# Half-wise drive buffers, reciprocals taken from a reshaped copy in memory, and a shorter end of the recall stage

## The chip, the cores and the metric

The kernel runs on one core of one Trainium2 chip. The metric is the device time of one execution in microseconds (us); lower is better. PE is TensorE (matmuls and transposes), PEld its weight loads, DVE VectorE, ACT ScalarE, POOL GpSimd, SP SyncE, which issues most DMAs.

## The reference

Eight images of 1024 tokens and 32 text tokens (`B` = 8, `SEQ` = 1056, width `D` = 64) pass through a Fourier patch embedding, attention, a mixture of 16 experts, a linear recurrent attention and a mixture of 8 experts. The change lies in the recurrent attention and at its seam to the last experts. Cut to what matters:

```python
def step(carry, v_prev):                       # over time, 1056 steps, n = 256 neurons
    x_update = relu(v_prev @ Dx.T)
    x_t = 0.97 * x_state + x_update
    x_t = x_t / max(sum(abs(x_t)), 1e-12)
    a_star = einsum('bdn,bn->bd', rho, x_t)
    y_t = relu(_ln(a_star) @ Dy.T) * relu(x_t)
    v_star = _ln(y_t @ E.T)
    rho_t = 0.97 * rho + _ln(v_prev)[:, :, None] * x_t[:, None, :]
    return (x_t, rho_t), v_star
h = h + _L1_attn_ref(_layernorm(h), E, Dx, Dy)
h = h + _L1_ffn_ref(_layernorm(h), ...)        # 8 experts, the best 2 of each token
```

## The kernel before

The program is a row of blocks with a barrier of all engines between two of them: nothing of a block starts before every engine has finished the block ahead. Inside a block each engine runs its own list in the order in which it is written, and waits on semaphores. Four blocks matter here.

**First experts** (`main` of `moe_phase`, tiles `d_...`), up to 1328 us. It ends before the input of the last two images is normalised.

**Drive** (`drive_block`). For each pair of images `pr` (0 to 3) the normalised rows are transposed on PE (`turn`, three pieces `i` through one bank `p_turn`) and copied by ACT (`keep`) into `vT`. For each of three chunks `a` of 352 columns PE forms `Dx @ v` (`drive`) into the four banks of `p_u`, and ACT applies the relu (`relu`) and writes `x_all`. `drive(pr, a)` fills all four banks at once: `p_u[:, q, f]`, `q` being the image of the pair and `f` the half of the 256 neurons; each `relu` reads the two banks of one image. DVE adds the two neuron halves (`join`), PE sums over neurons (`add_up`), and from that sum DVE works out the divisor of every time step (`level`, parts 0 to 7): a scaling, a comparison, a scan over time, two more operations, and four reciprocals of a quarter row each. It does so for images 0 and 1 here (`EARLY` = 2, rows on 2 partitions) and for images 2 to 7 (6 partitions) in the next block. SP writes the reciprocals to memory (`rate_scr`) and spreads them over 128 partitions (`spread_rate`), and DVE scans each image's half with them (`scan_drive`). On POOL `feed_drive(B - 1)` normalises the last image, after DVE has measured it (`feed_measure(g, dve, feed, 1, B - 1)` and `feed_gather`); PE's `turn(3, 0)` waits for it. The relus of the last pair wait for the end of the early levels, since these borrow rows of images 6 and 7.

**Recall** (`recall_answer_block`). A loop over `n`, with `b, t = divmod(n, 9)`, a tile of 128 tokens each: PE scores tile `n + 1` against itself, DVE masks it (`mask`, tile `k_pm`), PE weighs the values (`weigh`, tile `k_p_a`), and updates the state (`keep_state`). Score and mask buffers are two deep. Two images behind, `turn_la`, `core`, `gate` and `answer` make the output of image `b - 2`; DVE and POOL normalise and add it three images behind (`v_rows`, `v_moment`, `v_add`). In images 0 and 1 of the loop the cores and answers are still missing, and the late levels and the scans of images 1 to 3 stand in DVE's list. In its last rounds the block prepares image 0 of the second experts: `normalise`, `double`, `turn_tokens`, `logits`, `rank`, `choose`, `turn_gates`, `keep_gates`, then SP's `spread_out` and `spread_in` of the gates. POOL's last step is `v_add(7)`; the barrier waits for it.

**Second experts** (`main` of `moe_phase`, tiles `n_...`): 96 groups `i` of a first and a second layer on PE, from 1630 us to the end.

## Time and profile before

| | |
|---|---|
| median of 3 runs | 1944.66 us (1934.02 to 1953.28) |
| profiled execution, its own time | 1941.79 us |
| its span, first to last instruction | 1940.0 us |
| mean granted TensorE clock | 0.947 of full speed |
| PE busy | 1747.2 us (90%) |
| DVE, ACT, POOL busy | 1265.1, 1043.6, 348.9 us |
| first experts end, drive begins | 1328.8 us |
| drive ends, recall begins | 1390.7 us |
| recall ends, second experts begin | 1629.7 us |

All moments are counted from the first instruction of the profiled execution. Busy shares are means over stages with different limits; a change within drive and recall is to be read in the stretch from 1328 to 1634 us, and there in PE's idle time and its clock.

### The profile page before, as it was taken

To read this page: it belongs to the slowest core of one execution; us is meant where nothing else is said; L and a number is where in the kernel's file an instruction comes from. 1 tells how busy PE (TensorE), PEld (TensorE's weight loads), DVE (VectorE), ACT (ScalarE), POOL (GpSimd) and SP (SyncE) were. 2 spreads that over 40 slices of the span, in tenths; PEclk is the share of its full clock that TensorE was granted. 3 is DMA by queue.
4 is the path that set the end of the run, shared out by engine and by line. 5 is a ranking of instruction groups with operands and counts; after the bars stand their busy time and mean duration, and the time that the engine had idled before them with its cause. 6 is when DMAs were issued, how large, how long until landed. Compare 5 with 4: busy or idle time off the path is not lost. (4 is left out here: it accounts for less than half of the span.)

```text
span 1940.0 us, 41019 instructions
## 1 busy us (share of the span) xinstructions
PE 1747.2 (90%) x15480; PEld 756.6 (39%) x15480; DVE 1265.1 (65%) x3165; ACT 1043.6 (54%) x1974; POOL 348.9 (18%) x332
## 2 busy tenths in 40 slices
PE   5866899999999999999989999997899987999998
PEld 2331222222222222222324444443488974444443
DVE  1447888888888788878715687875666662434431
ACT  1330477777777677767764555554323332555554
POOL 1222100000000000000101345546113443000000
PEclk9975799999999899989999999998979997999999
DMA  5624022121212112110127576440110002332241
GB/s 189 230 76 73 2 35 47 35 46 36 45 37 42 40 34 48 29 36 19 35 63 155 105 135 131 92 91 18 34 58 13 1 2 46 71 79 52 58 87 22
DMA packets 89057, 118.74 MB, mean 61 GB/s; under 512 B 30892, under 2 KB 71942, under 8 KB 86814
## 3 DMA queue, kind: packets, MB, share of 16 engines
q1 hardware_dynamic: 84266, 106.93, 25.9%
q0 software_dynamic: 3104, 8.72, 1.3%
q8 instruction: 126, 2.06, 0.5%
q14 instruction: 69, 0.57, 0.1%
q10 hardware_dynamic: 1492, 0.46, 0.1%
HBM read 97.26 MB, written 18.82 MB: 60 GB/s over the span
## 5 line engine op out<-in xcount | busy, mean ns | idle before, releaser
L843 ACT ACTIVATE b_prob<-b_p_s 128x512 f32<-128x512 f32 x1104 | 570.4, 603 | 285.3 <-PE b_p_s L1012 269.8
L866 DVE TENSOR_REDUCE b_m<-b_p_m 128x1 f32<-128x1024 f32 x512 | 604.0, 1219 | 122.8 <-PE b_p_s L1012 87.7
L1012 PE MATMUL b_p_s<-b_q,b_k 51*64 51x512 bf16 x2048 | 347.9, 400 | 11.2 <-ACT b_prob L843 11.2
L967 PE MATMUL b_p_m<-b_k,b_q 48*64 48x512 bf16 x1656 | 301.5, 421 | 53.7 <-DMA b_k<-qk_scr 22.5
L1040 PE MATMUL b_p_o<-b_prob,v_all 128*9 128x512 f32 x2304 | 300.2, 603 | 0.9
L967 PEld LDWEIGHTS b_p_m<-b_k,b_q 48*64 48x64 bf16 x1656 | 75.1, 108 | 373.7 <-DVE b_m L866 233.2
L1414 ACT ACTIVATE d_hidden<-d_p_z 128x704 f32<-128x704 f32 x192 | 135.1, 754 | 103.0 <-PE d_p_z L1324 102.8
L1414 ACT ACTIVATE n_hidden<-n_p_z 128x704 f32<-128x704 f32 x192 | 135.0, 754 | 99.4 <-PE n_p_z L1324 99.2
L821 POOL DMA_DIRECT2D sum_scr<-b_sums x48 | 26.3, 548 | 747.5 <-ACT b_sums L833 723.7
L1552 DVE TENSOR_TENSOR d_xg<-d_xd,d_c_wide 128x352 f32<-128x352 f32 x192 | 113.1, 625 | 67.1 <-PE d_p_z L1324 32.9
L1324 PE MATMUL d_p_z<-d_xg,d_w 64*128 64x352 f32 x768 | 143.0, 488 | 0.6 <-DVE d_xg L1552 0.6
L1324 PE MATMUL n_p_z<-n_xg,n_w 64*128 64x352 f32 x768 | 142.2, 486 | 0.0
L1337 PE MATMUL d_p_y<-d_hidden,d_w 128*64 128x352 f32 x768 | 135.4, 474 | 0.0
L1337 PE MATMUL n_p_y<-n_hidden,n_w 128*64 128x352 f32 x768 | 134.6, 472 | 0.0
L1012 PEld LDWEIGHTS b_p_s<-b_q,b_k 51*64 51x64 bf16 x2048 | 92.0, 105 | 54.0 <-ACT b_prob L843 46.7
L1324 PEld LDWEIGHTS d_p_z<-d_xg,d_w 64*128 64x128 f32 x768 | 69.6, 188 | 48.9 <-ACT d_hidden L1414 23.1
L1324 PEld LDWEIGHTS n_p_z<-n_xg,n_w 64*128 64x128 f32 x768 | 69.3, 187 | 48.3 <-ACT n_hidden L1414 22.0
L1337 PEld LDWEIGHTS d_p_y<-d_hidden,d_w 128*64 128x64 f32 x768 | 47.0, 137 | 77.0 <-issue 63.3
L1552 DVE TENSOR_TENSOR n_xg<-d_xn_all,m_x_all 128x352 f32<-128x352 f32 x96 | 47.5, 518 | 44.8 <-PE n_p_z L1324 18.6
L1337 PEld LDWEIGHTS n_p_y<-n_hidden,n_w 128*64 128x64 f32 x768 | 46.7, 136 | 76.1 <-issue 62.3
L967 PE MATMUL b_p_m<-b_k_head,b_q_head 48*64 48x512 bf16 x392 | 63.1, 403 | 7.0 <-ACT b_prob L843 7.0
L2186 ACT ACTIVATE k_state<-k_p_r 128x128 f32<-128x128 f32 x64 | 17.7, 277 | 87.5 <-PE k_p_r L2111 86.6
(362 smaller groups left out, 2212.2 us busy)
## 6 DMA issues: line engine op xcount, KB each, us to landing
d_c_wide<-d_c_scr SPq DMA_DIRECT2D x48, 704.0 KB, 13.4
m_x_all<-n_c_scr SPq DMA_DIRECT2D x48, 352.0 KB, 8.2
xt<-in_x SPq DMA_DIRECT2D x16, 1024.0 KB, 8.7
sum_scr<-b_sums POOLq DMA_DIRECT2D x32, 256.0 KB, 2.8
b_q<-qk_scr SPq DMA_DIRECT2D x96, 66.0 KB
qk_scr<-a_qk_part SPq DMA_DIRECT2D x24, 256.0 KB, 2.8
k_rate<-rate_scr SPq DMA_DIRECT2D x8, 528.0 KB, 4.2
b_k<-qk_scr SPq DMA_DIRECT2D x16, 198.0 KB
```

What stands on the lines that cost most here:

```text
L821: pool.dma_start(g.sum_scr[b, p, :, a * WIDE:a * WIDE + w], sums[:, n % 2, 0:w]).then_inc(sum_sent[n % 2], 16)
L843: nc.scalar.activation(prob[:, U % PR_RING, 0:w], p_s[:, U % S_RING, 0:w], ACT.Exp, scale=float(D) ** -0.5).then_inc(exp_done, 1)
L866: nc.vector.tensor_reduce(m3[:, x, 0:1], p_m[:, s, :, :].rearrange("p k n -> p (k n)"), axis=AX.X, op=ALU.max).then_inc(rows_free, 1)
L967: last = nc.tensor.matmul(out[e:e + 64, k, :], q[:, t * P + e:t * P + e + 64], keys[:, k * WIDE:k * WIDE + WIDE], start=True, stop=True)
L1012: last = nc.tensor.matmul(out[e:e + 64, :], k_st[s][r, q, jt * P + e:jt * P + e + 64], q_st[s][r, q, a * WIDE:a * WIDE + WIDE], start=True ...
L1040: last = nc.tensor.matmul(p_o[32 * i:32 * i + DH + 1, :], v[:, jt, p * QUAD + i, :], prob[:, slot, :], start=(jt == 0), stop=(jt == FULL), ...
L1324: last = nc.tensor.matmul(own["p_z"][:, n % 2, q, 0:CH], w1[r, pr, f * P:f * P + P], own["xg"][r, n // HALVES % XR, :], start=True, stop=True)
L1337: last = nc.tensor.matmul(own["p_y"][q * D:q * D + D, 0:CH], w2[:, 2 * pr + q, f, :], own["hidden"][:, n % HR, q, :], start=(k == 0), stop ...
L1414: nc.scalar.activation(own["hidden"][:, n % HR, :, :], own["p_z"][:, n % 2, :, 0:CH], ACT.Relu).then_inc(relu_done, 1)
L1552: nc.vector.tensor_tensor(own["xg"][:, j % XR, :], own["xd"][b % 3][:, a * CH:a * CH + CH], own["c_wide"][b % 2][a][:, pr, :], ALU.mult)\
L2186: nc.scalar.mul(state[:, :, :].rearrange("p f d -> p (f d)"), p_r[:, 0:2 * D], DECAY ** -2).then_inc(held, 1)
```

## The change

Five things: (1) `drive(pr, a, f)` fills two banks, those of one neuron half, and `relu` reads them; PE fills the one half while ACT reads the other, with the transposes between the halves. (2) The levels stop after part 3. SP writes the divisors to memory and reads them back as rows of 66 elements on 32 (early) or 96 (late) partitions, DVE takes one reciprocal of that (`invert_levels`), SP writes it to `rate_scr`. (3) In drive, the statistics of the last image stand ahead of the levels, the scans of image 0 ahead of `join(6)` and `join(7)`, and `add_up(4)` and `add_up(5)` one chunk earlier. (4) In recall, the late levels fill rounds 0 to 3 in one row, the scans of image 1 move to rounds 4 and 6. (5) At recall's end both halves of `answer(6)` go ahead of `turn_la(7, ...)`, `normalise(1)`, `double(1)`, `turn_gates(0)` and `keep_gates(0)` go later, and the normalisation and addition of the last answer moves behind the barrier, into the second experts' block.

```diff
+            if answers:
+                answer_add(g, pool, answers, B - 1)
             rstd_of(2)
...
+                    if answers and i == 2:
+                        answer_rows(g, dve, answers, B - 1, range(NT))
+                    if answers and i == 3:
+                        answer_moments(g, dve, answers, B - 1)
+                    if answers and i == FIRST_GROUP[B - 1] - 4:
+                        dve.wait_ge(answers["v_step"], 5 * B)
...
+def load_levels(g, sp, k, lo, hi, level, part):
+    sp.wait_ge(k["level"], LEVEL_STEPS * (part + 1))
+    sp.dma_start(k["den_scr"][lo:hi, :], level).then_inc(k["den_sent"], 16)
+    sp.wait_ge(k["den_sent"], 16 * (part + 1))
+    sp.dma_start(k["den"][0:(hi - lo) * SPREAD, :], k["den_scr"][lo:hi, :].rearrange("b (s n) -> (b s) n", s=SPREAD)).then_inc(k["den_in"], 16)
+def send_rates(g, sp, k, rate_scr, lo, hi, part):
+    sp.wait_ge(k["inverted"], part + 1)
+    sp.dma_start(rate_scr[lo:hi, :].rearrange("b (s n) -> (b s) n", s=SPREAD), k["inverse"][0:(hi - lo) * SPREAD, :]).then_inc(k["rate_sent"], 16)
+    sp.wait_ge(k["rate_sent"], 16 * (part + 1))
+def invert_levels(g, dve, k, lo, hi, part):
+    dve.wait_ge(k["den_in"], 16 * (part + 1))
+    if part:
+        dve.wait_ge(k["rate_sent"], 16 * part)
+    n = (hi - lo) * SPREAD
+    g.nc.vector.reciprocal(k["inverse"][0:n, :], k["den"][0:n, :]).then_inc(k["inverted"], 1)
+LEVEL_STEPS = 6
+SPREAD = 16
...
-            def drive(pr, a):
-                n = NC * pr + a
+            def drive(pr, a, f):
+                n = 2 * (NC * pr + a) + f
                 pe.wait_ge(vT_ready, 3 * pr + 3)
-                pe.wait_ge(relu_done, 2 * n)
-                for f in range(2):
-                    for q in range(2):
+                if n >= 2:
+                    pe.wait_ge(relu_done, n - 1)
+                for q in range(2):
...
-                    drive(pr, a)
+                    drive(pr, a, 0)
                     if pr + 1 < TWOS:
                         turn(pr + 1, a)
+                    drive(pr, a, 1)
...
-                    if pr == 3 and a >= 1:
-                        add_up(3 + a)
+                    if pr == 3 and a < 2:
+                        add_up(4 + a)
...
-                    act.wait_ge(k["level"], LEVEL_STEPS)
+                    act.wait_ge(k["den_sent"], 16)
...
             join(0)
             join(1)
+            feed_measure(g, dve, feed, 1, B - 1)
+            feed_gather(g, dve, feed, 1, B - 1)
             dve.wait_ge(summed, EARLY)
             for part in (0, 1, 2):
                 level(part)
-            feed_measure(g, dve, feed, 1, B - 1)
-            feed_gather(g, dve, feed, 1, B - 1)
             join(2)
             level(3)
             join(3)
-            for part in (4, 5, 6, 7):
-                level(part)
-            for b in range(4, B):
-                join(b)
+            invert_levels(g, dve, k, 0, EARLY, 0)
+            join(4)
+            join(5)
             for f in range(2):
                 scan_drive(g, dve, k, u_all, 0, f)
+            join(6)
+            join(7)
...
-            for b in range(B + 3):
+            for b in range(B + 2):
...
-            pool.wait_ge(v_step, 5 * B)
...
+                if b == B and t == 7:
+                    for half in range(2):
+                        answer(b - 2, half)
...
+                if n == AFTER + 9:
+                    turn_gates(0)
...
-                if n == AFTER + 5:
+                if n == AFTER + 9:
                     normalise(1)
```

In drive, PE's list from the first product of pair 0 into pair 1 (`h_p_u` the drive, `h_p_turn` a transpose, `k_trio<-...f_column` an `add_up`), before:

```order
L1865 MATMUL h_p_u<-k_yT,k_xr 128x352 x4
L1855 MATMUL h_p_turn<-eye,d_xn_all 128x128 x4
L1865 MATMUL h_p_u<-k_yT,k_xr 128x352 x4
L1855 MATMUL h_p_turn<-eye,d_xn_all 128x128 x4
L1865 MATMUL h_p_u<-k_yT,k_xr 128x352 x4
```

and after the change:

```order
L1899 MATMUL h_p_u<-k_yT,k_xr 128x352 x2
L1889 MATMUL h_p_turn<-eye,d_xn_all 128x128 x4
L1899 MATMUL h_p_u<-k_yT,k_xr 128x352 x4
L1889 MATMUL h_p_turn<-eye,d_xn_all 128x128 x4
L1899 MATMUL h_p_u<-k_yT,k_xr 128x352 x4
```

The transposes stand inside a chunk now, after two of its four products; a row of four is the second half of one chunk and the first of the next.

In drive, DVE's list from the first two joins (`k_a_sb<-m_x_all`, `k_laT<-m_x_all`) to the barrier, before (`f_st`, `f_mv` the last image's statistics, `m_x_all<-m_x_all,k_rate` the scans of image 0):

```order
L1785 SCALAR_TENSOR_TENSOR k_v_sb<-k_rate,m_x_all 2x1056
L1684 BN_STATS f_st<-hid 128x6 x9
L1693 BN_AGGR f_mv<-f_st 128x2 x9
L1947 TENSOR_TENSOR k_a_sb<-m_x_all 128x1056
L1789 SCALAR_TENSOR_TENSOR m_x_all<-k_v_sb,m_x_all 2x1056
L1791 TENSOR_SCALAR m_x_all<-m_x_all 2x1056
L1947 TENSOR_TENSOR k_laT<-m_x_all 128x1056
L1795 RECIPROCAL k_rate<-m_x_all 2x264 x4
```

and after, the same stretch with what stands ahead of it:

```order
L1692 BN_STATS f_st<-hid 128x6 x9
L1701 BN_AGGR f_mv<-f_st 128x2 x9
L1792 TENSOR_SCALAR m_x_all<-k_trio 2x1056
L1793 MEMSET k_v_sb 2x1
L1796 TENSOR_SCALAR k_rate<-m_x_all 2x1056
L1799 SCALAR_TENSOR_TENSOR k_v_sb<-k_rate,m_x_all 2x1056
L1981 TENSOR_TENSOR k_a_sb<-m_x_all 128x1056
L1803 SCALAR_TENSOR_TENSOR m_x_all<-k_v_sb,m_x_all 2x1056
L1805 TENSOR_SCALAR m_x_all<-m_x_all 2x1056
L1981 TENSOR_TENSOR k_laT<-m_x_all 128x1056
L1829 RECIPROCAL k_inverse<-k_den 32x66
```

The statistics are ahead of the whole level, and one reciprocal of 66 elements a row stands where four of 264 stood.

At recall's end, PE's list from `core(6, 5)` to `core(7, 0)` (`k_trio<-eye,k_la` is `turn_la`, `k_eT,k_yT` is `answer`, `n_cw` is `turn_gates`), before:

```order
L2129 MATMUL k_p_s<-k_laT,k_dyT 128x352
L2120 MATMUL k_trio<-eye,k_la 64x128 x3
L2138 MATMUL k_trio<-k_eT,k_yT 128x64 x10
L2120 MATMUL k_trio<-eye,k_la 64x128 x3
L2138 MATMUL k_trio<-k_eT,k_yT 128x64 x8
L1298 MATMUL k_p_t<-eye,n_cw 64x128
L1299 MATMUL k_p_t<-eye,n_cw 8x128
L2120 MATMUL k_trio<-eye,k_la 64x128 x3
L2129 MATMUL k_trio<-k_laT,k_dyT 128x352
```

and after:

```order
L2181 MATMUL k_p_s<-k_laT,k_dyT 128x352
L2190 MATMUL k_trio<-k_eT,k_yT 128x64 x18
L2172 MATMUL k_trio<-eye,k_la 64x128 x9
L1300 MATMUL k_p_t<-eye,n_cw 64x128
L1301 MATMUL k_p_t<-eye,n_cw 8x128
L2181 MATMUL k_trio<-k_laT,k_dyT 128x352
```

Both halves of answer 6 stand ahead of the three transposes of image 7, and the transposes of the gates behind them.

## Rows read from the trace of the kernel before

**Rows 1.** Stretch, length, busy PE, PEld, DVE, ACT, POOL, granted clock, DMA share, GB/s

```profile
1328.80:1390.50 61.70, 47.67 (x192) 21.37 (x192) 34.06 (x74) 24.61 (x43) 20.39 (x16) 0.85 0.12 32
1391.00:1403.00 12.00, 11.77 (x103) 11.34 (x103) 10.44 (x13) 5.31 (x14) 1.56 (x4) 1.00 0.21 46
1403.00:1415.00 12.00, 8.97 (x73) 7.51 (x71) 11.66 (x21) 3.61 (x11) 0.00 (x0) 1.00 0.01 3
1417.00:1431.00 14.00, 14.00 (x67) 13.92 (x66) 3.93 (x7) 2.60 (x8) 1.35 (x1) 0.50 0.35 116
1596.50:1608.40 11.90, 10.20 (x47) 9.10 (x47) 3.21 (x35) 2.34 (x7) 5.75 (x5) 0.50 0.02 5
```

**Rows 2.** Timeline of drive: start us, us, engine, line, operation, idle before

```profile
1343.38 2.30 POOL L1725 TENSOR_TENSOR hid<-hid,d_xn_all 128x576 f32<-128x576 f32 x1
1343.82 1.46 PE L1865 MATMUL h_p_u<-k_yT,k_xr 64*128 64x352 f32 x8 [1.39 <-ACT k_yT L1913]
1345.20 0.66 PE L1855 MATMUL h_p_turn<-eye,d_xn_all 128*128 128x128 f32 x4
1345.32 1.41 ACT L1919 ACTIVATE m_x_all<-h_p_u 128x704 f32<-128x704 f32 x2 [1.55 <-PE h_p_u L1865]
1353.85 1.20 DVE L1684 BATCH_NORM_STATS2 f_st<-hid 128x6 f32<-128x64 f32 x9
1358.14 0.70 DVE L1791 TENSOR_SCALAR m_x_all<-m_x_all 2x1056 f32<-2x1056 f32 x1
1362.42 1.09 PE L1855 MATMUL h_p_turn<-eye,d_xn_all 128*128 128x128 f32 x4 [5.38 <-POOL d_xn_all L1710]
1388.52 1.94 PE L1872 MATMUL k_trio<-k_laT,f_column 128*6 128x352 f32 x6
```

**Rows 3.** SP's issues of the early rates, and DMA issue to landing

```profile
1366.73 0.23 SPq L1832 DMA_DIRECT2D rate_scr<-k_rate  x1
1368.11 0.82 SPq L1762 DMA_DIRECT2D k_rate<-rate_scr  x2
DMA to landing us min/median/max: 3.6/4.2/5.5
```

**Rows 4.** The late reciprocals on DVE: min/median/max in ns, first and last start

```profile
L1795 DVE RECIPROCAL k_yT<-k_yT x4: 1792/1792/1793, 1405.6 to 1412.4; 6x264 f32<-6x264 f32 x4
```

**Rows 5.** Timeline of recall's first two images: weighing on PE, DVE

```profile
1396.01 0.33 PE L2099 MATMUL k_p_a<-v_all,k_pm 128*128 128x64 f32 x2
1397.79 0.33 PE L2099 MATMUL k_p_a<-v_all,k_pm 128*128 128x64 f32 x2
1415.21 0.53 PE L2099 MATMUL k_p_a<-v_all,k_pm 128*128 128x64 f32 x2 [0.73 <-DVE k_pm L2250]
1418.63 0.53 PE L2099 MATMUL k_p_a<-v_all,k_pm 128*128 128x64 f32 x2
1436.04 2.35 DVE L1767 TENSOR_TENSOR_SCAN m_x_all<-m_x_all,k_rate 128x1056 f32<-128x1056 f32 x1
1442.06 0.28 DVE L2250 TENSOR_TENSOR k_pm<-k_p_s,k_tri 128x128 f32<-128x128 f32 x1
```

**Rows 6.** Timeline of recall's end and the start of the second experts

```profile
1592.16 0.76 DVE L1471 TENSOR_TENSOR v_all<-v_all,n_rs 128x576 f32<-128x576 f32 x1 [1.97 <-POOL n_rs L1252]
1596.54 0.85 PE L2120 MATMUL k_trio<-eye,k_la 128*64 128x128 f32 x3 [5.08 <-DVE k_la L2284]
1608.41 1.54 PE L2129 MATMUL k_trio<-k_laT,k_dyT 128*128 128x352 f32 x2 [0.56 <-ACT k_laT L2191]
1616.22 0.21 POOL L2037 TENSOR_TENSOR k_v_mv<-k_v_mv,eps 128x9 f32<-128x9 f32 x1 [10.21 <-DVE k_v_mv L2296]
1620.89 1.40 POOL L2045 TENSOR_TENSOR hid<-hid,k_v_sb 128x576 f32<-128x576 f32 x1
1627.84 1.40 POOL L2045 TENSOR_TENSOR hid<-hid,k_v_sb 128x576 f32<-128x576 f32 x1
1629.97 1.11 PE L1283 MATMUL n_p_g<-eye,m_x_all 128*128 128x128 f32 x4 [10.15 <-POOL n_yT L1255]
```

More of the change, by code:

```diff
@@ L1553, in scale, with main @@
                     .then_inc(gated, 1)
-        def main():
+        def main(answers):
             scale(0)
@@ L1599, in vector_steps, with main @@
         return measure, gather, normalise, rank, choose, main
-    def main(chunks, stale):
+    def main(chunks, stale, answers=None):
         with ExitStack() as c2:
@@ L1629, in _ @@
                 _, _, _, run = pool_steps(pool)
-                run(stale)
+                run(stale, answers)
             @block.tensor
@@ L1644, in _ @@
                 _, _, _, _, _, run = vector_steps(dve)
-                run()
+                run(answers)
     return own, main, (sync_steps, pool_steps, tensor_steps, scalar_steps, vector_steps)
@@ L1744, in feed_recall, with recall_buffers @@
     feed_normalise(g, pool, feed, 2, n + 3, feed["vn"][:, b, :, :], feed["sums"][b])
-def recall_buffers(g, c):
+def recall_buffers(g, c, late):
     sb = lambda n, s: c.enter_context(g.nc.sbuf_tensor("k_" + n, s, F32))
+    keep = lambda n, s: late.enter_context(g.nc.sbuf_tensor("k_" + n, s, F32))
+    v_sb, v_st, v_mv = keep("v_sb", [P, 2, NT, D]), keep("v_st", [P, NT, 6]), keep("v_mv", [P, NT, 4])
     return {"rate": sb("rate", [P, RATES, SEQ]), "tri": sb("tri", [P, P]), "fade": sb("fade", [P, 2, NT]),
@@ L1791, in level_of @@
         nc.vector.tensor_scalar(scaled, scaled, L1_EPS / DECAY, None, ALU.max).then_inc(step, 1)
-    if part >= 4:
-        dve.wait_ge(step, n0 + 6)
-        cols = slice((part - 4) * SEQ // 4, (part - 3) * SEQ // 4)
-        nc.vector.reciprocal(small[:, cols], scaled[:, cols]).then_inc(step, 1)
-LEVEL_STEPS = 10
+def load_levels(g, sp, k, lo, hi, level, part):
[15 more added lines that the diff above has]
+SPREAD = 16
 def drive_block(g, u_all, feed, rate_scr, k, p_sum, own, steps):
@@ L1830, in _ @@
             load_experts()
-            sp.wait_ge(k["level"], LEVEL_STEPS)
-            sp.dma_start(rate_scr[0:EARLY, :], early["small"]).then_inc(rate_sent, 16)
-            sp.wait_ge(rate_sent, 16)
+            load_levels(g, sp, k, 0, EARLY, early["scaled"], 0)
+            send_rates(g, sp, k, rate_scr, 0, EARLY, 0)
             for b in range(EARLY):
@@ L1926, in _ @@
                 for a in range(NC):
-                    for q in range(2):
-                        relu(pr, a, q)
+                    relu(pr, a, 0)
                     if pr + 1 < TWOS:
                         keep(pr + 1, a)
+                    relu(pr, a, 1)
                     if (pr, a) == (1, 1):
@@ L2010, in _ @@
             load_biases()
-            sp.wait_ge(kb["level"], 2 * LEVEL_STEPS)
-            sp.dma_start(rate_scr[EARLY:B, :], late["small"]).then_inc(rate_sent, 16)
-            sp.wait_ge(rate_sent, 16)
+            load_levels(g, sp, kb, EARLY, B, late["scaled"], 1)
+            send_rates(g, sp, kb, rate_scr, EARLY, B, 1)
             for b in range(EARLY, B):
@@ L2228, in _ @@
                     soften(0)
-                if n == AFTER + 8:
-                    keep_gates(0)
                 if 1 <= b <= B and t >= 7:
@@ L2234, in _ @@
                     laT_copy(b - 2, 2)
+                if n == AFTER + 9:
+                    keep_gates(0)
                 if b < B:
@@ L2305, in _ @@
             mask(0)
-            for n in range(NT * (B + 3)):
+            for n in range(NT * (B + 2)):
                 b, t = divmod(n, NT)
@@ L2320, in _ @@
                     gather(1)
-                if n == AFTER + 5:
+                if n == AFTER + 9:
                     normalise(1)
@@ L2419, in all_stages @@
         with ExitStack() as c3:
-            buffers = recall_buffers(g, c3)
+            buffers = recall_buffers(g, c3, c)
             trio = c3.enter_context(nc.psum_tensor("k_trio", [P, 3, 512], F32))
@@ L2423, in all_stages @@
             recall_answer_block(g, x_all, vn_all, rate_scr, feed, buffers, trio, own, steps)
-        second_experts((), ())
+        second_experts((), (), buffers)
 def build(nc, arg, const, out, stages):
```

111 lines of the change are left out of this document (54 added, 57 removed).

## The prediction

> **What bounds the kernel now.** I read the busy shares by stretch first, then the timeline of PE's waits, then DVE, POOL and SP around them. The experts and the attention stage, some 1600 of the 1940 us, keep PE busy and are not touched. The change lies where PE waits. Drive lasts 61.7 us and PE is busy for 47.67 of them, so 14.0 us are idle, and the clock's mean of 0.85 says that it stood at 1.2 GHz for three tenths of the stretch [rows 1]. Recall's first two images are bound by DVE from 1403 to 1415 (DVE 11.66 of 12.00 us busy, PE 8.97), and right after that the clock stands at 1.2 GHz with PE busy without a gap, 14.00 of 14.00 us [rows 1]. At recall's end PE waits for DVE, runs at 0.50 [rows 1], and idles while POOL adds the last answer; those numbers follow below.
>
> **Drive: buffers by half.** Before, a chunk's four products take 1.46 us and the two relus behind them 1.41 us, one after the other, since PE needs all four banks back: the row of 1343.82 shows PE waiting 1.39 us for ACT, and ACT in turn waiting 1.55 us for PE [rows 2]. With halves, PE has 1.46 + 0.66 (four transposes) = 2.1 us a chunk and ACT its relus and a copy of about the transposes' length, 1.41 + 0.6 = 2.0 us, beside each other. Only the two joins' `add_up` (1.94 us each) still hold PE for data. **The moved statistics.** The last image is ready on POOL at 1343.38 + 2.30 = 1345.7, but DVE measures it at 1353.85, behind the level's scan, and PE waits 5.38 us for POOL's result, until 1362.42 [rows 2]. Put ahead of the level, the measuring starts at about 1346, so POOL is done after the same 1362.42 - 1353.85 = 8.6 us, at 1354.6, or sooner, since the two instructions that ran slowly there ran beside DVE's joins. PE gets there at about 1353. The price is 2 us more before the level; as `add_up(1)` ends only at about 1348, DVE would have waited through those 2 us anyway.
>
> **Drive: the levels through memory.** The early level is ready for the reciprocals at 1358.14 + 0.70 = 1358.8 [rows 2], and the rates leave at 1366.73 [rows 3]: 7.9 us, of which a join and four reciprocals. Written over 32 partitions a row has 66 elements, a quarter of 264. At the duration per element of the late ones, 1.79 us for 264 [rows 4], one reciprocal of 66 takes an estimated 0.45 us; from below it is not under the 0.28 us of a mask [rows 5], from above not over 1.79. It adds two DMAs, out and back. The only row alike is the write of the rates, 1368.11 - 1366.73 = 1.4 us until SP was released [rows 3]; the read may take up to the 4.2 us of a landing [rows 3], though it moves 8 KB and not 528. I take 1.4 + 2.0 + 0.5 = 3.9 us in place of 6.9 on this path. The level itself comes some 3 us earlier, at 1355.7, as its sum does. Rates then land at 1355.7 + 3.9 + 1.4 + 4.2 = 1365.2. The relus of the last pair no longer wait for reciprocals, only for the first write (1357).
>
> **Drive: the sum.** Walked through in the new order, with `add_up(1)` ending at 1348 (pair 0 runs mostly at the low clock and gains about 1 us) and the other two chunks of pair 1 at 1352: pair 2 takes three chunks of 2.1 and two `add_up` of 1.94, 10.2 us, to 1362; pair 3, without transposes, three of 1.46 and two of 1.94, 8.3 us, to 1370; DVE's two scans (2.35 us each, [rows 5]) run from 1366 to 1371 and are through when the last relus end (1371); joins 6 and 7 to 1374; `add_up(7)` ends at 1378 instead of 1388.52 + 1.94 = 1390.5 [rows 2]. **Drive gives 12 us.** By the other way round: 14.0 us idle less about 4 that stay (the first copies, the joins) and plus 2 of a cold stretch that no longer occurs is the same 12. Bounds 8 (halves worth nothing beyond the moved statistics and level) and 15 (no idle left, no low clock but the first).
>
> **Recall's start.** DVE's list loses four reciprocals of 1.79 us, 7.2 us, and gains 0.45. The scans of image 1 move behind the level. Between two masks at most 2.4 us of other work stand, three times in a row (rounds 2 to 4), against PE's pace of 1397.79 - 1396.01 = 1.78 us a tile [rows 5]: with buffers two deep that costs about 1 us once. Before, PE lost 12.00 - 8.97 = 3.0 us there [rows 1], so 2 us are saved at the least. The rest hangs on the clock. The tiles come every 1418.63 - 1415.21 = 3.42 us after the fall and 1.78 before [rows 5]. The fall came after the stretch in which PE was busy for 75%; the twelve us before it, of the same tiles at 98%, kept 2.4 GHz [rows 1]. Without the gaps I expect it to stay. Then DVE becomes the bound at rounds 15 to 18: four scans of 2.35 us, the centring and scaling, statistics and masks, about 13 us for what PE does in 8. Followed through, the mask that stands at 1442.06 [rows 5] comes 10 us earlier, not 14. **I take 10**, bounds 3 (clock falls as before) and 13. The late rates pass three DMAs of 1.4 to 4.2 us and one spread of 4.2; the scan that needs them is six rounds, 11 us, behind the reciprocal, so they cost nothing.
>
> The Trainium skill's page "TensorE: Matmul & The Clock Gate", part 1, says that sustained activity releases the throttle; by that the stretch from 1417 would have been short, and this term only 2 us. The trace doesn't agree: the clock stayed at 0.50 through 14.00 us without an idle moment [rows 1].
>
> **Recall's end.** `normalise(1)` no longer stands ahead of the last gates, so DVE doesn't wait 1.97 us for POOL there [rows 6]; with its own two instructions of 0.76 gone, what stands behind comes 3.5 us sooner, gate (6, 5) near 1593. PE's 5.08 us of idling [rows 6] shrink to some 1.6, then answer 6 fills PE, and the three transposes of image 7 with their copies are no longer held up by ACT's `keep_gates`, which waited for the gates' transposes. `core(7, 0)` starts at 1605 instead of 1608.41 at the low clock, at 1601 if it stays high. From it the last gate takes the 7 us of before, then DVE's moments, and POOL's addition of answer 6: 1616.22 to 1620.89 + 1.40 = 1622.3, 6.1 us [rows 6]. That is now the end: 1619 (low) or 1613 (high), where before POOL went on to 1627.84 + 1.40 = 1629.2 [rows 6]. So 10 or 16 us; 6.9 of them are the last addition alone. I take **10**, since the clock was already low in [rows 1] at 1596.5 and a pause of 1.6 us behind a thin stretch may suffice. The addition in the next block costs PE nothing: DVE has about 2 us more and POOL 6.1, and the next statistics that POOL must finish come two groups (6 us) later than the moments. SP's gates leave about as early as before and the first chunk has landed when the block starts; bound 2 us.
>
> **Sum.** 1941.8 - 12 - 10 - 10 = 1909.8. The profiled execution is 2.9 us below the median of three, which spread by 19 us, so I make it **1910 us**.
>
> **Rivals.** (a) *The clock falls in recall's start anyway*, say because most of these products move only 64 columns: the term is 3 and not 10, 1917 us. For it: at 0.50 the same tiles, without a gap, brought no rise in 14 us [rows 1]; against it: the 98% stretch. Chance 0.33 against 0.37 for the forecast. The same page, part 4, says that transposes don't count as busy in the same way, and recall is full of them; that speaks for this rival, and no run here parts transposes from thin products. (b) *The clock stays high at the end too*: 6 us more and a warm start of the experts, 1903 us; chance 0.17. (c) *Halves don't do what they say*: PE in drive is held by joins, levels and rates, not by buffers; drive gives 8 or less, 1914 to 1918; chance 0.08. (d) *Slower*: the clock, low from a place in recall on, does not come back with the products of 352 columns. Each tile at 3.42 and not 1.78 costs 1.64 us, so from 32 / 1.64 = 20 low tiles more than before it eats everything. Images 2 to 7 have them in every tile; 0.02. (e) The round trips through memory take the reciprocals' place as the wait: each us beyond the 1365 of the rates delays the scans, joins 6 and 7 and the barrier by the same; at 4.2 us each for three DMAs drive gives 6; 1916, chance 0.03.
>
> **The numbers.** Range 1896 to 1925: from (b) with drive at 15 to (a) with drive at 8, and the spread of the runs. About 1% (19 us) is what a measurement of this kernel can tell from no change. All cases but (d) and an unforeseen one lie below 1925; with both terms of the clock at their worst and the early bounds (8 + 3 + 7 = 18) it is within 1%. Faster 0.92, same 0.06, slower 0.02.
>
> **What would show it.** In drive: ACT's and PE's rows overlapping, no wait of PE on POOL, last `add_up` at about 1378. In recall: no run of waits of PE on `k_pm` in the first nine tiles, clock 1.0 at 35 to 40 us from recall's start; one 96-row reciprocal of about 0.5 us. At the end: the barrier about 10 us after the last gate's core, PE's idle time ahead of the second experts 3 to 4 us and not 10.15. The forecast is wrong if the clock falls at another place, or if DVE's rows of statistics in the experts make PE wait.

## The result, and the profile after

| | before | changed |
|---|---|---|
| median | 1944.2 us (4 runs, 1934.0 to 1953.3) | 1917.8 us (4 runs, 1915.1 to 1926.4) |
| ratio to before, 95% interval | | 0.9858 [0.9815, 0.9900] |
| span of the profiled execution | 1940.0 us | 1914.3 us |
| drive, first transpose to recall's first DMA issue | 61.9 us | 55.1 us |
| recall, to the second experts' first product | 239.2 us | 217.2 us |
| ... its start to the mask of tile 20 | 51.3 us | 41.3 us |
| ... from there to the last mask | 135.3 us | 135.3 us |
| ... from the last mask to the second experts | 52.7 us | 40.6 us |
| second experts | 310.0 us | 311.2 us |

The spans differ by 25.7 us: 6.8 in drive, 22.1 in recall, less 1.2 lost in the second experts and 2.1 by which the unchanged blocks ahead of drive were later in this execution. The forecast was 1910 in 1896 to 1925. The gain is 1.4%, and the interval of the ratio lies below 1. Here and below the ratios leave out a few executions that ran at a lower clock, so that they are not always the quotient of the medians.

Busy time by stretch in the changed kernel, columns as in [rows 1]: drive, recall's two first twelve us, the low stretch, the end.

```profile
1330.80:1385.90 55.10, 47.39 (x192) 19.71 (x192) 29.89 (x71) 25.43 (x43) 23.39 (x16) 0.86 0.13 36
1386.30:1398.30 12.00, 11.77 (x103) 11.25 (x102) 9.75 (x13) 5.31 (x14) 1.50 (x4) 1.00 0.22 48
1398.30:1410.30 12.00, 11.60 (x104) 10.91 (x103) 7.07 (x30) 4.53 (x14) 2.02 (x2) 1.00 0.32 95
1418.00:1424.00 6.00, 6.00 (x29) 5.15 (x30) 4.62 (x7) 2.18 (x6) 0.00 (x0) 0.50 0.24 90
1580.00:1592.00 12.00, 10.65 (x42) 8.11 (x42) 3.80 (x20) 3.43 (x8) 6.29 (x5) 0.51 0.01 4
```

Drive has 7.7 us of idle PE in place of 14.0, but the mean clock is 0.86 and not near 1. Its timeline, which answers to [rows 2]:

```profile
1346.33 2.29 POOL L1733 TENSOR_TENSOR hid<-hid,d_xn_all 128x576 f32<-128x576 f32 x1
1352.96 4.14 POOL L1716 TENSOR_TENSOR d_xn_all<-hid,f_mv 128x576 f32<-128x576 f32 x1
1357.17 2.06 POOL L1718 TENSOR_TENSOR d_xn_all<-d_xn_all,f_mv 128x576 f32<-128x576 f32 x1
...
1352.57 2.35 DVE L1799 TENSOR_TENSOR_SCAN k_v_sb<-k_rate,m_x_all 2x1056 f32<-2x1056 f32 x1
1354.84 1.22 DVE L1981 TENSOR_TENSOR k_a_sb<-m_x_all 128x1056 f32<-128x1056 f32 x1
1355.99 2.21 DVE L1803 SCALAR_TENSOR_TENSOR m_x_all<-k_v_sb,m_x_all 2x1056 f32<-2x1056 f32 x1
1358.23 1.56 DVE L1805 TENSOR_SCALAR m_x_all<-m_x_all 2x1056 f32<-2x1056 f32 x1
...
1359.38 1.09 PE L1889 MATMUL h_p_turn<-eye,d_xn_all 128*128 128x128 f32 x4 [4.42 <-POOL d_xn_all L1718]
```

PE still waits 4.42 us for POOL, and the four transposes behind the wait take 1.09 us and not 0.66: the clock fell to 0.50 during the wait, at 1356.3, and was back at 1363.1. POOL's subtraction took 4.14 us and its multiplication 2.06; DVE's operations beside them are long too (L1805 1.56 us, before 0.70). In the kernel before, POOL's four operations on this image, two narrow ones and the same two wide ones, were:

```profile
1355.92 1.08 POOL L1700 TENSOR_TENSOR f_mv<-f_mv,eps 128x9 f32<-128x9 f32 x1 [10.24 <-issue]
1357.08 2.70 POOL L1702 TENSOR_TENSOR f_mv<-f_mv,minus_half 128x9 f32<-128x9 f32 x1
1359.86 1.17 POOL L1708 TENSOR_TENSOR d_xn_all<-hid,f_mv 128x576 f32<-128x576 f32 x1
1361.11 1.17 POOL L1710 TENSOR_TENSOR d_xn_all<-d_xn_all,f_mv 128x576 f32<-128x576 f32 x1
```

There the narrow two were the slow ones (0.21 and 1.81 us in the changed kernel); the wide two took 1.17 us each, as the last of the joins ended.

The round trip of the early levels, and the late reciprocal, in answer to [rows 3] and [rows 4] (SP's issues in drive; then DVE by line and form, with busy us and mean ns):

```profile
1359.82 0.23 SPq L1811 DMA_DIRECT2D den_scr<-m_x_all  x1
1361.20 0.31 SPq L1813 DMA_DIRECT2D k_den<-den_scr  x1
1363.41 0.31 SPq L1819 DMA_DIRECT2D rate_scr<-k_inverse  x1
1364.76 0.81 SPq L1776 DMA_DIRECT2D k_rate<-rate_scr  x2
```

```profile
L1829 DVE RECIPROCAL k_inverse<-k_den 96x66 f32<-96x66 f32 x1 | 0.6, 553 | 0.0
```

From the level's end to the rates' departure it is 3.6 us, 3.9 in the forecast and 7.9 before. In recall (PE, then the mask of tile 20 on DVE) and at its end:

```profile
1417.35 0.52 PE L2172 MATMUL k_trio<-eye,k_la 128*64 128x128 f32 x3 [1.77 <-DVE k_la L2339]
...
1427.25 0.28 DVE L2305 TENSOR_TENSOR k_pm<-k_p_s,k_tri 128x128 f32<-128x128 f32 x1
...
1577.84 7.67 PE L2190 MATMUL k_trio<-k_eT,k_yT 128*128 128x64 f32 x36 [1.12 <-DVE k_yT L2313]
...
1589.56 1.54 PE L2181 MATMUL k_trio<-k_laT,k_dyT 128*128 128x352 f32 x2
...
1603.12 1.12 PE L1285 MATMUL n_p_g<-eye,m_x_all 128*128 128x128 f32 x4 [1.78 <-POOL n_yT L1255]
...
1601.18 1.39 POOL L2022 TENSOR_TENSOR hid<-hid,k_v_sb 128x576 f32<-128x576 f32 x1
...
1611.26 1.40 POOL L2022 TENSOR_TENSOR hid<-hid,k_v_sb 128x576 f32<-128x576 f32 x1
```

PE's idle time ahead of the second experts is 1.78 us where [rows 6] had 10.15. The last addition on POOL, at 1611.26, lies in the next block, beside PE's work.

### The profile page after: what moved, and what is told of

Same layout as the page of the kernel before. It is cut to its first block and busy times, and to the rows that moved or that the text cites. A ratio compares the mean times of both kernels' runs of the same rounds, so it can differ in the third digit from the quotient of the medians.

```text
span 1914.3 us, 41028 instructions
## 1 busy us (share of the span) xinstructions
PE 1741.5 (91%) x15480; PEld 748.2 (39%) x15480; DVE 1254.4 (66%) x3159; ACT 1044.5 (55%) x1974; POOL 352.1 (18%) x332
## 3 DMA queue, kind: packets, MB, share of 16 engines
q8 instruction: 126, 2.06, 0.5%
## 5 line engine op out<-in xcount | busy, mean ns | idle before, releaser
L967 PE MATMUL b_p_m<-b_k,b_q 48*64 48x512 bf16 x1656 | 301.3, 420 | 53.8 <-DMA b_k<-qk_scr 22.5
L1040 PEld LDWEIGHTS b_p_o<-b_prob,v_all 128*9 128x9 f32 x2304 | 37.5, 89 | 69.9 <-issue 54.0
```

The costliest lines, as they stand in the source:

```text
L967: last = nc.tensor.matmul(out[e:e + 64, k, :], q[:, t * P + e:t * P + e + 64], keys[:, k * WIDE:k * WIDE + WIDE], start=True, stop=True)
L1040: last = nc.tensor.matmul(p_o[32 * i:32 * i + DH + 1, :], v[:, jt, p * QUAD + i, :], prob[:, slot, :], start=(jt == 0), stop=(jt == FULL), ...
```

## The experiments

All twelve kernels are the changed one with one thing undone or altered, or two or three (runs 10 and 12). A median of four to six runs moves by several us with the unchanged blocks: drive began between 1328.8 and 1341.2 us in the fourteen profiled executions. So the verdicts go by the length of stages, each read from one profiled execution. In recall it repeats: in the kernels that leave its start as it is, the mask of tile 20 came 41.3 or 41.4 us behind recall's first issue (40.9 in one). In drive it repeats less well.

| kernel | median us | ratio to before | drive | to tile 20 | last mask to experts | recall | second experts |
|---|---|---|---|---|---|---|---|
| before | | | 61.9 | 51.3 | 52.7 | 239.2 | 310.0 |
| changed | 1917.8 | 0.9858 [0.9815, 0.9900] | 55.1 | 41.3 | 40.6 | 217.2 | 311.2 |
| 1 halves undone | 1919.8 | 0.9892 [0.9864, 0.9919] | 52.6 | 41.3 | 40.5 | 217.9 | 309.8 |
| 2 statistics back | 1917.6 | 0.9863 [0.9844, 0.9882] | 57.9 | 41.3 | 40.6 | 217.1 | 311.2 |
| 3 reciprocals back | 1932.2 | 0.9925 [0.9895, 0.9955] | 56.3 | 54.3 | 41.4 | 232.0 | 311.2 |
| 4 last addition back | 1923.2 | 0.9909 [0.9885, 0.9932] | 54.8 | 41.4 | 47.8 | 224.3 | 310.5 |
| 5 DVE quiet | 1918.4 | 0.9868 [0.9835, 0.9901] | 55.4 | 41.4 | 40.3 | 216.8 | 311.2 |
| 6 normalised on DVE | 1915.2 | 0.9829 [0.9798, 0.9860] | 50.5 | 41.3 | 40.6 | 217.4 | 311.2 |
| 7 scans apart | 1920.1 | 0.9842 [0.9814, 0.9871] | 56.4 | 39.9 | 41.6 | 217.0 | 309.8 |
| 8 transposes later | 1917.8 | 0.9879 [0.9805, 0.9954] | 50.3 | 41.3 | 40.6 | 217.4 | 311.2 |
| 9 scaling ahead | 1915.5 | 0.9811 [0.9769, 0.9853] | 54.2 | 37.1 | 40.6 | 213.2 | 309.6 |
| 10 = 1 and 6 | 1918.0 | 0.9825 [0.9777, 0.9873] | 51.8 | 40.9 | 41.7 | 217.6 | 309.8 |
| 11 order undone | 1926.5 | 0.9866 [0.9829, 0.9903] | 53.8 | 41.3 | 45.5 | 222.4 | 309.8 |
| 12 = 6, 8 and 9 | 1914.2 | 0.9843 [0.9816, 0.9870] | 51.1 | 37.1 | 41.5 | 214.1 | 311.2 |

Drive's code is the same in the changed kernel and in runs 4, 7, 9 and 11: 53.8 to 56.4 us. Part of that spread goes with POOL's subtraction, which took 2.9 us in runs 9 and 11 (drive 54.2 and 53.8) and 4.1 in the others (54.8 to 56.4). A difference of a us or two between two drives is within it. By their ratios only run 3 differs from the changed kernel, and run 4 barely, both longer; what the other runs show is shown in stages alone.

**1. Halves undone.**

```diff
-                    drive(pr, a, 0)
+                    drive(pr, a)
                     if pr + 1 < TWOS:
                         turn(pr + 1, a)
-                    drive(pr, a, 1)
```

> The changed kernel with one part undone: a chunk's four products are issued together again and each relu reads both neuron halves of one image. Everything else stays changed. Drive lasted 55.0 us in the changed kernel, from its first transpose to recall's first issue by SP, and 61.9 before. Theory A: the wait for POOL sets the time of pair 3 and the halves act only in pairs 1 and 2, where each of some three chunks saves about 1 us: drive 57 to 58 us, whole kernel 2 to 3 us above the changed one. Theory B, the step of the prediction (halves overlap PE and ACT in every chunk): 5 to 6 us, drive 60 us or more. Theory C, the prediction's rival (c): joins, levels and POOL hold PE and the halves are worth nothing: drive within 0.5 us of 55.0.

Drive was 2.5 us *shorter*, which none of the theories had. PE's rows with and right behind the last chunk of pair 2 that waits, then POOL's:

```profile
1363.76 1.45 PE L1899 MATMUL h_p_u<-k_yT,k_xr 64*128 64x352 f32 x8 [1.40 <-ACT k_yT L1947]
1365.36 0.63 PE L1889 MATMUL h_p_turn<-eye,d_xn_all 128*128 128x128 f32 x4
...
1359.88 3.18 POOL L1716 TENSOR_TENSOR d_xn_all<-hid,f_mv 128x576 f32<-128x576 f32 x1
1363.13 2.08 POOL L1718 TENSOR_TENSOR d_xn_all<-d_xn_all,f_mv 128x576 f32<-128x576 f32 x1
```

POOL is slow here too, but PE, held up for 1.0 and 1.4 us at a time by ACT, comes to `turn(3, 0)` when POOL is just done: no wait, full clock. With halves PE saves these small waits, gets there earlier, idles 4.42 us in one piece and then works at half clock. The new wait took back what the halves had gained. That it cost more than that rests on one profiled execution, 1.2 us below the lowest drive with halves and with the wait; its subtraction took 3.18 us and not 4.14, and the median of the kernel, 1919.8, does not show the gain.

**2. The statistics of the last image behind the level again.** The two `feed_` lines of `vector` move back behind `level(2)`.

> The changed kernel with one part undone: in drive the statistics of the last image stand behind parts 0 to 2 of the level again, as before the change. Theory A: PE's transposes of pair 3 wait for POOL, and POOL for these statistics; PE gets the image 4 to 6 us later, POOL's two wide instructions take nearer 1.2 us each since they run at other moments than DVE's scan, so 3 to 4 us of it are left: drive 58 to 59 us in place of 55.0. Theory B: the two us that the level loses by standing behind the statistics, and the slow POOL, eat what the move brings: drive 55 to 56 us.

```profile
1363.87 1.08 PE L1889 MATMUL h_p_turn<-eye,d_xn_all 128*128 128x128 f32 x4 [7.33 <-POOL d_xn_all L1718]
...
1361.30 1.17 POOL L1716 TENSOR_TENSOR d_xn_all<-hid,f_mv 128x576 f32<-128x576 f32 x1
1362.55 1.17 POOL L1718 TENSOR_TENSOR d_xn_all<-d_xn_all,f_mv 128x576 f32<-128x576 f32 x1
```

57.9 us, close to theory A, though the image comes 2.9 us later and not 4 to 6: PE waits 2.9 us more, and 2.8 us are lost. The two wide instructions, which here run when DVE has a join behind it and then waits for a DMA, take 1.17 us each.

**3. Reciprocals on DVE again**, 2 x 4 of 264 elements, no round trips:

```diff
-            invert_levels(g, dve, k, 0, EARLY, 0)
+            for part in (4, 5, 6, 7):
+                level(part)
...
-                if n == 8:
-                    invert_levels(g, dve, kb, EARLY, B, 1)
+                if n in (5, 7, 8, 9):
+                    level({5: 4, 7: 5, 8: 6, 9: 7}[n])
```

> The changed kernel with one part undone: eight reciprocals on DVE of 264 elements a row in place of the two round trips through memory with one reciprocal of 66 each; the late ones stand in rounds 5, 7, 8 and 9 of recall. Theory A (what the prediction says of DVE's list): in drive DVE is busy 7.2 us more from 1361 on, the relus of the last pair wait for them until about 1368, and drive is 4 to 5 us longer; in recall DVE's list grows by 6.6 us where DVE sets the pace, of which 5 to 6 show up at the mask of tile 20. Together 9 to 11 us. Theory B: since the rates landed 4 us before their scan and the clock falls in recall anyway, the reciprocals cost 2 us or less in each of the two places, 4 us together.

In drive 1.3 us, within the spread of that code; in recall 14.8, of which 13.0 by tile 20, twice what DVE's list grew by. PE's longest waits in the 6 us before the clock fell, then the stretches of recall behind the fall:

```profile
1407.54 0.43 PE L2158 MATMUL k_p_a<-v_all,k_pm 128*128 128x64 f32 x2 [0.40 <-DVE k_pm L2312]
1409.69 0.43 PE L2158 MATMUL k_p_a<-v_all,k_pm 128*128 128x64 f32 x2 [0.58 <-DVE k_pm L2312]
...
1411.00:1425.00 14.00, 13.33 (x63) 12.50 (x63) 9.46 (x28) 3.28 (x10) 2.02 (x2) 0.50 0.22 70
1425.00:1440.00 15.00, 14.51 (x72) 14.19 (x71) 6.23 (x10) 3.06 (x9) 0.00 (x0) 0.50 0.12 47
```

The clock was at 1.2 GHz from 1410.5 to 1448.1 here, from 1415.4 to 1439.3 before, from 1417.7 to 1424.6 in the changed kernel. In all twelve kernels in which it fell here it came back in the same place of the program, in round 18 or at the start of 19, 0.5 to 1.9 us ahead of the first `core` product. What differs is where it fell: at DVE's first congestion. Neither theory had the size; the full rounds are paid once in waiting and again in every tile until then. The size is that of the profiled execution, the longest of six: three took 1937 to 1939 us and three 1924 to 1928. If drive began in the shortest one no earlier than in any profile (1328.8), all that follows took at most some 10 us more than in the changed kernel (an estimate from the spans), and not 16; no profile shows that case.

**4. The last addition ahead of the barrier again** (`answer_rows`, `answer_moments` and `answer_add` of image 7 back in recall's loops).

> The changed kernel with one part undone: the rows, moments and addition of the last answer stand ahead of the barrier again, in recall's block. The order of answer 6, of the transposes and of normalise(1) stays changed. Theory A: recall's end is POOL's addition of the last answer, so the second experts' block starts 6 to 7 us later, and the block itself is some 1 us shorter, since its start is 1.2 us longer in the changed kernel than before: 5 to 6 us in all. Theory B: the addition lies beside copies and statistics that the barrier waits for anyway, or the block gives the time back: 2 us or less.

```profile
1607.26 1.40 POOL L2014 TENSOR_TENSOR hid<-hid,k_v_sb 128x576 f32<-128x576 f32 x1
...
1609.38 0.90 PE L1283 MATMUL n_p_g<-eye,m_x_all 128*128 128x128 f32 x3 [10.16 <-POOL n_yT L1255]
```

Recall 7.2 us longer, the next block 0.7 shorter, 6.5 in all: theory A, a little above its 5 to 6.

**5. DVE quiet while POOL normalises.**

```diff
             dve.wait_ge(summed, EARLY)
+            dve.wait_ge(feed["step"][1], FEED_STEPS[1] * B)
```

> The changed kernel with one wait added: in drive DVE begins the early level only when POOL has finished the last image. In the changed kernel POOL's subtraction took 4.14 us and its multiplication 2.06 beside DVE's scan, join and level; where DVE was idle or waiting, the same two took 1.17 each. Theory A (POOL's wide instructions are slowed by DVE's work beside them): both fall to about 1.2 us, PE's wait of 4.42 us for POOL falls to about 1, and since the level comes some 5 us later and is not what PE waits for, drive is 1 to 3 us shorter than 55.1. Theory B (the 4.14 us are of another cause, the rows that POOL reads or its own code): they stay over 2.5 us each or together, and drive is 3 to 5 us longer, by the delayed level.

```profile
1352.58 1.17 POOL L1716 TENSOR_TENSOR d_xn_all<-hid,f_mv 128x576 f32<-128x576 f32 x1
1353.82 1.17 POOL L1718 TENSOR_TENSOR d_xn_all<-d_xn_all,f_mv 128x576 f32<-128x576 f32 x1
...
1358.24 1.55 PE L1899 MATMUL h_p_u<-k_yT,k_xr 64*128 64x352 f32 x4 [5.28 <-ACT k_yT L1948]
```

The same two instructions on the same data take 1.17 us each with DVE idle, 4.14 and 2.06 with DVE at work: the slowing is shown. But drive was not shorter, against theory A. I had not counted ACT: its `mul` of the early sums, behind chunk (1, 1), waits for the level's first part, so with the level 4.9 us later ACT stood, and PE waited 5.28 us for ACT's copy in place of 4.42 for POOL.

The Trainium skill's page "SBUF — State Buffer", section "SBUF: two separate sides", says that VectorE and GpSimd share a port pair as an exclusive lock: an operation of VectorE with two inputs in SBUF, or in one of its two-port modes, and one of GpSimd that reads SBUF keep each other out for a whole instruction. The rows of the changed kernel agree for the operations with two inputs: POOL's subtraction, issued at 1352.96 during DVE's scan, ends at 1357.10, 1.0 us after the join that ends at 1356.06, and DVE's next operation of two inputs, begun at 1355.99, ends at 1358.20, 1.1 us after POOL. `L1805`, which has one input, was slowed as well; whether it ran in a two-port mode no row shows.

**6. The last image normalised on DVE.**

```diff
-            for part in (0, 1, 2):
-                level(part)
+            level(0)
+            level(1)
+            nc.vector.tensor_tensor(x, g.hid[:, B - 1, :, :], wide(mv[:, :, 0:1]), ALU.subtract)
+            nc.vector.tensor_tensor(x, x, wide(mv[:, :, 2:3]), ALU.mult)
+            level(2)
```

> The changed kernel with one part altered: the subtraction and the multiplication of the last image in drive are done by DVE, between parts 1 and 2 of the level, and not by POOL. Theory A (drive is set by PE's wait for the last image, and that wait is what makes the clock fall): DVE needs 0.8 us for each, PE has the image about 4 us earlier, the clock stays at 1.00, drive is 5 us shorter, 50 us. Theory B (joins and rates set drive behind it): the wait goes but the joins take its place, drive 54 us.

```profile
1356.48 0.76 DVE L2001 TENSOR_TENSOR d_xn_all<-hid,f_mv 128x576 f32<-128x576 f32 x1 [0.39 <-POOL f_mv L1710]
1357.28 0.76 DVE L2003 TENSOR_TENSOR d_xn_all<-d_xn_all,f_mv 128x576 f32<-128x576 f32 x1
...
1361.49 1.94 PE L1907 MATMUL k_trio<-k_a_sb,f_column 128*6 128x352 f32 x6 [1.60 <-DVE k_a_sb L1982]
```

50.5 us, as theory A had it. No wait for the image, 1.60 us for a join, full clock (a sum still takes 1.94 us).

**7. The scans of images 2 and 3 further apart** (rounds 13, 15, 18, 21).

> The changed kernel with one part altered: in recall the scans of image 2 stand in rounds 13 and 15, not 15 and 16, and those of image 3 in rounds 18 and 21, not 17 and 18. In the changed kernel DVE is full in rounds 15 to 18, PE's weight loads are busy for 2.23 of 4 us, and right behind that the clock falls to 0.50 for about 8 us. Theory A (the fall comes from PE's waits there, as in the prediction): the clock stays at 1.00 up to 45 us from recall's start, and the mask of tile 20 and the end of recall come 3 to 4 us earlier. Theory B (the thin products of the first two images are what makes the clock fall, as in rival (a)): it falls at 30 us from recall's start as now, and the time is within 1 us.

```profile
1423.20:1427.20 4.00, 2.23 (x24) 2.05 (x22) 3.29 (x5) 0.76 (x3) 0.00 (x0) 1.00 0.10 35
1427.20:1431.20 4.00, 4.00 (x26) 3.21 (x25) 0.80 (x5) 2.16 (x6) 0.00 (x0) 0.64 0.28 105
...
1426.54 0.52 PE L2172 MATMUL k_trio<-eye,k_la 128*64 128x128 f32 x3 [1.77 <-DVE k_la L2339]
```

Between the theories: the clock still fell, 33 us from recall's start for 32 in the changed kernel, and was back after some 3 us; tile 20 came 1.4 us earlier, and recall as a whole gave it back (217.0). The wait was still the same 1.77 us: `turn_la(0, 0)` needs the scaling of image 0, which stands behind a scan.

**8. The transposes of the last pair one chunk later** in PE's and ACT's lists.

```diff
                     if pr < 2:
                         turn(pr + 1, a)
+                    if pr == 2 and a:
+                        turn(3, a - 1)
```

> The changed kernel with one part altered: in drive the three pieces of transposes of the last pair stand one chunk later in PE's list, so that four products and a sum lie ahead of the wait for POOL. In the run with the halves undone PE came to POOL's result late, waited not at all, kept the clock at 1.00, and drive took 52.6 us in place of 55.1. Theory A (the idle wait for POOL brings the clock down, and that costs more than the wait): the wait falls from 4.42 us to 1 to 2, the clock stays at 1.00 behind the first stretch, drive 52 to 53 us. Theory B (the sum 2 and the products wait for DVE and ACT just as long): the wait only changes its name and drive is 55 us or more.

```profile
1367.35 1.94 PE L1906 MATMUL k_trio<-k_a_sb,f_column 128*6 128x352 f32 x6 [1.35 <-DVE k_a_sb L1989]
...
1370.01 0.66 PE L1889 MATMUL h_p_turn<-eye,d_xn_all 128*128 128x128 f32 x4
```

50.3 us, better than expected: POOL is still slow (2.92 and 2.06 us), but PE has products and a sum ahead of the wait, finds the image ready and keeps 2.4 GHz. Runs 1, 6 and 8 remove the wait in three ways, and in all three the low clock behind it goes too.

**9. Scaling of image 0 ahead of the scans.**

```diff
+                if n in (NT + 3, NT + 4):
+                    (la_centre if n == NT + 3 else la_scale)(0)
+                if n in (NT + 5, NT + 6):
+                    scan(2, n - NT - 5)
+                if n in (18, 21):
+                    scan(3, (n - 18) // 3)
```

> The changed kernel with one part altered, in recall: the two scans of image 3 stand in rounds 18 and 21 as in the run before it, and the centring and scaling of the first image's recalled values stand in rounds 12 and 13, ahead of the two scans of image 2 in rounds 14 and 15. With only the scans moved PE still waited 1.77 us for that scaling, PE's weight loads were busy 2.05 of 4 us, the clock fell behind it for about 3 us in place of 8, and tile 18 was masked 36.8 us from recall's start in place of 38.2. Theory A (PE's idle time in this place brings the clock down): with the scaling early the wait goes, the clock stays at 1.00 throughout the first 60 us of recall, tile 18 is masked at 34 to 35 us and tile 27 at 60 to 61, not 63.6. Theory B (another cause lies behind it, such as the thin products): a fall at 28 to 32 us again, and tile 27 at 62 or later. Either way the time of recall as a whole need not follow, since e7 gave its 1.2 us back by the end.

```profile
1416.20:1420.20 4.00, 3.63 (x35) 3.42 (x34) 3.40 (x4) 1.88 (x5) 0.00 (x0) 1.00 0.02 4
1420.20:1424.20 4.00, 4.00 (x36) 3.51 (x35) 2.86 (x7) 2.25 (x7) 0.00 (x0) 1.00 0.37 135
```

Theory A: the wait is gone (0.37 us is the longest in this place), the clock stays at 1.00 on the same thin products, tile 20 comes 4.2 us earlier and recall is 4.0 us shorter. So the thin products do not bring the clock down by themselves; PE's idle time among them does. They still have a part: in run 3 the clock fell here behind waits of 0.40 and 0.58 us, while in drive of run 1 it stayed over waits of 1.01 and 1.40 us ahead of products of 352 columns.

**10. Whole buffers with DVE's normalisation.**

> The changed kernel with two alterations: all four products of a chunk together (halves undone, as in the first run) and the last image's subtraction and multiplication on DVE. It asks what halves are worth once nothing waits for POOL: with halves and DVE's normalisation drive took 50.5 us. Theory A (halves overlap PE and ACT in every chunk and were hidden by the wait for POOL and its clock): 2 to 3 us longer than that, 53 us. Theory B (joins and scans set drive, halves are worth nothing): 50 to 51 us.

51.8 against 50.5 us: with the wait for POOL gone, halves give 1.3 us, between the theories. It is one profiled execution of each, and the same drive code has differed by 2.6, so the sign is likely and the size is not shown. PE still waits 1.0 and 1.4 us for ACT in turn, but with halves it waits for the joins instead (1.60 us in run 6).

**11. The order of recall's end undone.**

> The changed kernel with one part undone: at recall's end answer 6 stands half by half behind the transposes of image 7, and normalise(1), double(1), turn_gates(0) and keep_gates(0) where they stood before; the last addition stays in the second experts' block. From recall's start to the second experts took 217.15 us in the changed kernel, 224.3 with only the addition undone, 239.2 before, of which 10 were gained by tile 20. Theory A (the order is worth what is left of the gain behind tile 20, some 5 us, while the late addition gives 7): 222 us. Theory B (the order gives nothing by itself, the 5 us come from elsewhere, such as a clock that stays high in the middle of recall): 217 to 218 us.

```profile
1588.25 0.85 PE L2172 MATMUL k_trio<-eye,k_la 128*64 128x128 f32 x3 [5.09 <-DVE k_la L2336]
...
1600.12 1.54 PE L2181 MATMUL k_trio<-k_laT,k_dyT 128*128 128x352 f32 x2 [0.56 <-ACT k_laT L2243]
```

5.2 us in recall, 5.0 of it between the last mask and the experts, as theory A had it. With the 7.2 us of run 4 this makes the 12.1 of the result, within 0.1. PE's 5.09 us of idling is back [rows 6], and the clock stands at 1.2 GHz for 20.4 us at recall's end (20.5 before) and not for 13.6 as in the changed kernel.

**12. Runs 6, 8 and 9 together.**

> The changed kernel with three alterations taken together: the last image's subtraction and multiplication in drive on DVE, the transposes of the last pair one chunk later in PE's list, and in recall the scaling of the first image ahead of the scans of image 2, with those of image 3 in rounds 18 and 21. Alone they gave drives of 50.5 and 50.3 us in place of 53.8 to 56.4, and a recall of 213.2 us in place of 217.2. Theory A (each removes its own wait, and the two in drive the same one): drive 50 us, recall 213 us, the rest as it was, 9 us below the changed kernel, a ratio to the kernel before of 0.981. Theory B (the order in drive adds to DVE's normalisation): drive 48 us. Theory C (recall's gain was luck of one run): recall 217 us.

```profile
1334.90:1386.00 51.10, 45.38 (x192) 19.16 (x192) 29.47 (x73) 25.20 (x43) 17.19 (x14) 0.92 0.15 38
1386.00:1446.00 60.00, 57.58 (x486) 53.79 (x486) 45.38 (x134) 22.44 (x65) 16.91 (x18) 1.00 0.18 57
```

Drive 51.1, recall 214.1: 7 us less than the changed kernel in the two stages, clock 1.00 through recall's first 60 us. It is faster than the kernel before (0.9843), but the 9 us that theory A gave it over the changed kernel did not come: the medians, 1914.2 and 1917.8, do not tell the two apart, and in the profiled executions the unchanged blocks ahead of drive took 4 us more here. In drive the two alterations do not add up: DVE's two instructions of 0.76 us now delay the join that PE waits for (2.23 us, 1.35 in run 8), so run 8 alone does as well.

## Why the prediction was right, and where it was off

The time, 1917.8, lies in the range and 7.8 us above the point; the terms were 12, 10 and 10, measured 6.8, 10.0 and 12.1, and 1.2 lost behind. Of the 7.8, drive gives 5.2, the next block 1.2, the unchanged blocks 2.1, recall's end takes back 2.1, and the rest is that the profiled execution lies 1.7 below the median. That the end covered part of drive's error is luck.

- **Drive, forecast 12, measured 6.8.** The step that failed is that POOL is done "at 1354.6, or sooner, since the two instructions that ran slowly there ran beside DVE's joins". The two that ran slowly before were the narrow ones, 1.08 and 2.70 us beside DVE's joins, and they did get faster (0.21 and 1.81). I did not see that the moved level, with its scan, and a join would now stand beside the two wide ones, which had taken 1.17 us each. The measuring began 17.8 us into drive, as forecast (before 25.0), but POOL needed 10.6 us from there and not 8.6 or less; its two wide instructions took 6.2 us of that, 2.3 when alone (run 5). From that followed the wait of 4.42 us and the low clock behind it, which the forecast held to be gone ("a cold stretch that no longer occurs"). With the wait removed (runs 6 and 8) drive gives 11.4 and 11.6 us, close to the 12. In such kernels the next wait is near: in runs 8 and 10 DVE's first scan starts 0.02 us after its rates land, where the changed kernel has 4.6 us to spare.
- **Halves.** They overlap PE and ACT as said, but give little: 1.3 us (runs 6 and 10) once nothing waits for POOL, within the spread of drive, and nothing or a loss in the kernel as it stands (run 1: 52.6 us without them, 53.8 to 56.4 with them). Rival (c) had the drive at 8 or less and the time at 1914 to 1918, which is what came, at a chance of 0.08; but its reason, that joins and levels hold PE, holds only for a part.
- **The moved statistics** were worth 2.8 us (run 2; 1.5 to 4.1 against the spread of that code).
- **The levels through memory.** Path 3.6 us for 3.9, reciprocal 0.55 for 0.45; the rates landed 4.6 us ahead of their scan, so rival (e) is out for this kernel. (The 6.9 us that the prediction sets against its 3.9 are the four reciprocals alone; with the join ahead of them the path was 7.9. The sum does not use them.) On DVE the reciprocals cost recall 14.8 us in the profiled execution of run 3, and the medians lie 14.4 us apart. This is the part that carries the change.
- **Recall's start, forecast 10, measured 10.0**, but by another path. The forecast had a clock that stays high and DVE as the bound in rounds 15 to 18. DVE was the bound there, PE idled 1.77 us, and the clock did fall, as in rival (a); it cost little, since it fell some 7 us before the place where it comes back, and not 24. Neither the forecast nor rival (a), which priced the fall at 7 us, had asked when it comes back. That the term is 10.0 all the same is luck: without the fall it is 14.2 (run 9, with the scans moved too). Run 9 shows that the forecast's mechanism (without gaps it stays) is right and that the gap was one instruction's place in DVE's list. The transposes, which the prediction counted for rival (a), are all in that list of PE's too, at 1.00.
- **Recall's end, forecast 10, measured 12.1:** the addition 7.2 for 6.9, the order 5.0 for 3.1, with 7 us less of low clock in it. The clock was low, as taken, and rival (b) is out.
- **The next block.** A loss of 1.2 us against a bound of 2. Its length goes with the mean granted clock of its first 6 us: 0.72 or 0.73 in the five kernels with 309.6 to 309.8 us, 0.68 before (310.0), 0.57 in run 4 (310.5), 0.50 to 0.53 in those with 311.2. Runs 1, 7, 9, 10 and 11 have the moved addition in this block and are 0.2 to 0.4 us shorter than the kernel before at nearly its clock, so the addition costs nothing that shows. That the loss is the clock's is read from these rows and not tested alone.
- **Rival (d)** is out: the low clock came back by round 19 each time.

No run takes apart what else the change moved: in drive the scans of image 0 ahead of two joins and the two sums one chunk earlier, in recall the rounds of the late levels and of image 1's scans. Run 3 puts the early and the late reciprocals back together. What stays open too is why the clock comes back in round 18 or 19. The Trainium skill's page "TensorE: Matmul & The Clock Gate", part 1, says that sustained activity releases the throttle; run 3 shows 29 us at 0.50 with PE busy for 27.8 of them and no rise, so here that rule alone does not tell when the clock returns.

## What to carry to other kernels

A part that makes PE faster ahead of a fixed wait can gain nothing, since it turns scattered short waits into one long one and the clock falls with it; before moving or speeding anything, find the longest single wait that is left and put work ahead of it (run 8: 4.8 us for moving three groups of transposes). When a step is moved on DVE, look at what POOL does at the new moment, and count both engines' operations there at their slow rows. Judge such parts by the length of their stage, and profile the same code more than once before trusting a us or two: drive moved by 2.6 us with unchanged code, the start of drive by 12.
